# Latent attention with lookback: projection behind the second scores, mask on GpSimd, last key's values by DMA, two evictions on ScalarE

## The chip, the cores and the metric

The kernel runs on one core of one Trainium2 chip. The metric is the device time of one execution of the whole program, in microseconds (us); lower is better. Below, PE is TensorE, DVE is VectorE, ACT is ScalarE, POOL is GpSimd and SP is SyncE, as the profile names them.

## What is computed

The program is a stack of six layers on activations `x` of 64 x 32 tokens of 256 features: an adapter attention, a self attention, a ternary feed-forward, the latent attention that the change is about, a gated attention and a layer of experts. Only the fourth is touched. For each of the 64 batches it takes 32 query tokens and 257 context tokens (`ctx_2048`), 16 heads, and computes, with the context as 257 keys:

```python
kv_c = kv @ W_kvc                     # 256 -> 64
q_c = q @ W_dq                        # 256 -> 96
q_nope, q_rope = q_c @ W_uq, rope(q_c @ W_qr)
k_nope, v, k_rope = kv_c @ W_uk, kv_c @ W_uv, rope(kv_c @ W_kr)
scores = (q_nope . k_nope + q_rope . k_rope) / sqrt(192)
good = (k_ids <= seg_id) & (k_ids >= seg_id - 8)
attn = softmax(where(good, scores, -1e30))
out = (attn @ v) @ W_o
```

The up-projections of keys and values are folded into those of the queries and of the output, so that a batch has one key tile of 128 rows (64 of the latent, 64 rotary) and its values are the latent rows themselves, turned. All of it is in fp32.

## The kernel before

The order of work is written out by hand, engine by engine, with semaphores; there is no planner. `latent_attention` (line 1149) holds one function for each engine: `sp`, `pool`, `scalar`, `vector`, `tensor`. After a prologue (weights, folding, norm of x, latent queries `d_qcT`), all of them walk through 64 steps, one for a batch `b`, by `steps` (line 1234): steps 0 to 3 and 52 to 63 written out, 4 to 51 in a loop of eight steps. Four batches are a tile of 128 rows of x; the 16 heads are four groups, scored two at a time (u = 0 and u = 1). Every engine takes its instructions strictly in the order of its queue, and a wait holds all that is behind it.

TensorE's step b (line 1602) is in this order: first scores of b (L1566); second half of the weighting of b-2 (L1582); turning the first two groups' probabilities of b-1 (L1548); `values` of b, which turns the latent keys into values by two transposes (L1537) and copies the last key to four rows by a small product (L1539); keys of b+1 (L1515); in every fourth step (b mod 4 = 1, from 5) the output projection `project` of the tile before (L1591, 16 passes); second scores of b (L1566); `turn_last` of b-1, the last key's probabilities (L1556); queries of b+5 (L1525); turning the second two groups of b-1 (L1548); and the weighting of b-1, which starts with the last key (L1577) and then takes the first half (L1582). Keys and queries go through one bank of PSUM, so the queries of b+5 wait until VectorE has taken the keys of b+1 out.

VectorE's step (line 1439) makes the mask of the batch (`window`, L1434, from the distances of ScalarE), takes out the first scores with mask and maximum (L1421, L1423, negated maximum L1427), evicts the values (`values_out`: L1396 for the 256 keys, L1397 for the last key spread over a 4 x 4 diagonal), takes the keys of b+1 out with their rotary parts (L1375, L1377), takes out the second scores (L1427 again), adds the projection to x in every fourth step (L161 and the statistics L135), evicts the last key's turned probabilities (`last_out`, L1405) and takes the queries of b+5 out (L1386, L1388).

ScalarE's step (line 1325): exponentials of the first two groups (L1335), scaling of the second two groups of b-1 (L1316), output of b-2 out of PSUM (L1324), turned probabilities of b-1 out (L1309), exponentials of the second two groups, turned probabilities again, scaling of the first two groups of b, distances of b+1 (L1301). GpSimd adds the rotary halves of keys (L1251) and queries (L1256). SyncE loads the context of b+2 when the keys of b have left its buffer (L1230, in a loop).

In TensorE's queue `turn_last(b - 1, 1 - j, b)` waits for the values of b to have been evicted, and the weighting waits for the last key's probabilities:

```python
            def turn_last(b, j, values):
                pe.wait_ge(scaled.sem, scaled.at(b, 2))
                pe.wait_ge(v_out.sem, v_out.at(values, 1))
            ...
            def weigh(b, j, u):
                if u == 0:
                    pe.wait_ge(t3_out.sem, t3_out.at(b, 1))
```

Of the kernel before, what the change touches and what calls it, by code (L numbers as in the profile page):

```python
# [83 lines left out]
def build(nc, d, out):  # L84
# [1064 lines left out]
    def latent_attention(sb):  # L1149
# [20 lines left out]
        own3 = sb("d_own3", [G1, G1])  # L1170
# [7 lines left out]
        wm = sb("d_wm", [P, LC])  # L1178
# [11 lines left out]
        w_loaded = shared("w_loaded", 16 * 14, 1)  # L1190
# [4 lines left out]
        ctx_loaded = [shared(f"ctx_loaded{j}", 16, B // 2) for j in range(2)]  # L1195
        k_psum, k_half, k_ready = shared("k_psum", 1, B), signal("d_k_half"), signal("d_k_ready")
# [5 lines left out]
        wm_link, dist_ready = chain("d_wm_link", 1), signal("d_dist_ready")  # L1202
# [15 lines left out]
        def sp(eng):  # L1218
            for dst, name in ((wdq[:], "d_wdq"), (wuq[:], "d_wuq"), (wuk[:], "d_wuk"), (wuv[:], "d_wuv"),
                              (wo[:], "d_wo"), (wkvcT[:], "d_wkvcT"), (wkr[:], "d_wkr"),  # L1220
                              (qw[:, :, KVC:P], "d_wqr"), (own3[:], "d_own3"),
# [5 lines left out]
            with eng.Fori(1, B // 2) as i:  # L1227
                for j in range(2):
                    eng.wait_ge(k_psum.sem, k_psum.at(i * 2 + (j - 1), 0))
                    eng.dma_start(cT[j][:, :, :], d["ctx"][i * 2 + j]).then_inc(ctx_loaded[j].sem, 16)  # L1230
# [15 lines left out]
        def pool(eng):  # L1246
            low = slice(KVC, P)

            def key_sum(b, j):
                eng.wait_ge(k_half.sem, k_half.at(b, 1))  # L1250
                eng.tensor_tensor(kc[j][low, :], kc[j][low, :], ks[low, :], ALU.add).then_inc(k_ready.sem, 1)  # L1251

            def query_sum(n, s, g):

                eng.wait_ge(q_half.sem, q_half.at(n, 1))
                eng.tensor_tensor(qc[s][low, g, :, :, :], qc[s][low, g, :, :, :], qs[low, :, :, :], ALU.add)\  # L1256
                    .then_inc(q_ready.sem, 1)

            def step(b, s, tile, pair):
                if not (isinstance(b, int) and b == B - 1):  # L1260
                    key_sum(b + 1, (s + 1) % 2)
                if not (isinstance(b, int) and b >= B - AHEAD):
                    query_sum(b + AHEAD, (s + AHEAD) // BT % 2, (s + 1) % BT)

            key_sum(0, 0)
            for piece in range(AHEAD):
                query_sum(piece, piece // BT, piece % BT)
            steps(eng, step)

        def scalar(act):  # L1270
# [27 lines left out]
            def distances(b, j, first):  # L1298
                if not first:
                    act.wait_ge(wm_link.sem, b - 1)  # L1300
# [11 lines left out]
            def scale(b, j, u):  # L1312
# [4 lines left out]
                ins.then_inc(scaled.sem, 1)  # L1317

# [34 lines left out]
            for u in range(2):  # L1353
                turn_out(B - 1, u)
            output_out(B - 1, 7, NT - 1)

        def vector(dve):
# [5 lines left out]
            seg_link.link(dve, dve.tensor_scalar(segf[:, :], segf[:, :], LOOKBACK / 2, -1.0, ALU.subtract, ALU.mult))  # L1363
            with dve.Fori(0, NT // 2) as i:
# [27 lines left out]
            def values_out(b, j, first):  # L1392
                dve.wait_ge(v_psum.sem, v_psum.at(b, 1))
                if not first:
                    dve.wait_ge(pv_psum.sem, pv_psum.at(b - 1, 0))
                dve.tensor_copy(vc[j][:, :, :], ps[:, T_BANK[1], P:2 * P].rearrange("p (c e) -> p c e", c=2))  # L1396
                dve.tensor_tensor(v3[j][:, :, :], spread(ps[0:G1, T_BANK[1], 2 * P:2 * P + KVC], 1, G1),  # L1397
# [1163 lines left out]
```

## Time and profile before

| what | value |
| --- | --- |
| median of 3 runs | 3097.93 us (3092.5 to 3103.39) |
| the profiled execution's own time | 3107.65 us |
| its span, first to last instruction | 3105.8 us |
| granted TensorE clock over the span | 0.859 |
| fourth layer, from its first weight load to its last statistics | 1494 to 2211 us |
| its 64 steps, from the first to the last first-scores eviction | 1572 to 2197 us |

A row of a group of instructions has: line, engine, operation, out<-in by the program's names, shapes, count | busy us, mean ns of one | idle time of the engine before them and what ended it. A row of the timeline has: start, duration, engine, line, operation, names, count, and in brackets the idle time before it and what released it. The granted clock is 1.00 at 2.4 GHz and 0.50 at 1.2 GHz.

### The profile page before, as it was taken

The numbers are of one execution on the slowest core, as the hardware profiler recorded it, in microseconds if no ns is written. First come the engines' busy times: TensorE is split into PE (matmuls) and PEld (weight loads), VectorE is DVE, ScalarE is ACT, GpSimd is POOL, SyncE is SP. The second block draws the span as 40 slices with busy tenths as digits, with TensorE's granted clock in tenths as the row PEclk, the third lists the DMA queues.
The fourth block names the chain that finished last, engine by engine and source line by source line (L and its number), as shares of the span: only waits on it lengthen the run. The fifth ranks groups of instructions, "written<-read, shape, count | busy, mean of one in ns | idle before, by whom it ended". The sixth has DMA issues, their size and how long they took to land.

```text
span 3105.8 us, 53176 instructions
## 1 busy us (share of the span) xinstructions
PE 2305.6 (74%) x15563; PEld 1566.6 (50%) x15596; DVE 2027.5 (65%) x5626; ACT 1390.6 (45%) x3648; POOL 585.0 (19%) x634
## 2 busy tenths in 40 slices
PE   5699999999999783232578888888777445566555
PEld 4666666666666552111356666666555322233222
DVE  3356666666666455666267777776377787777777
ACT  1054555544554343232235555555455544444444
POOL 0011111111111000111021222211144442222222
PEclk9999999999999896676789999999778657766777
DMA  2010100000000001000201011011000220000000
GB/s 79 0 25 24 23 24 24 24 24 24 24 24 9 15 0 51 0 0 0 75 21 28 28 28 26 26 27 28 20 10 10 90 79 1 1 1 1 1 1 28
DMA packets 62257, 71.38 MB, mean 23 GB/s; under 512 B 39802, under 2 KB 41275, under 8 KB 59580
## 3 DMA queue, kind: packets, MB, share of 16 engines
q1 hardware_dynamic: 62140, 70.20, 7.7%
q14 instruction: 89, 0.73, 0.1%
q8 instruction: 28, 0.46, 0.1%
HBM read 63.20 MB, written 2.10 MB: 21 GB/s over the span
## 4 chain that ended last, share of the span: by engine, by line
PE 47%; issue 23%; DVE 19%; ACT 7%; DMA 1%; DVEq 1%; SPq 1%; POOL 1%; ACTq 0%; POOLq 0%
PE ps L613 5%; PE ps L660 5%; PE ps L591 4%; PE ps L600 4%; PE ps L627 4%; PE ps L563 2%; DVE d_st L1423 2%; PE ps L1945 2%; PE ps L1120 2%; PE ps L672 1%; ACT d_pr L1316 1%; PE ps L671 1%; DVE x_all L161 1%; PE ps L861 1%; PE ps L1566 1%
## 5 line engine op out<-in xcount | busy, mean ns | idle before, releaser
L350 ACT ACTIVATE a_pr<-ps,a_nm 128x257 f32<-128x257 f32 x512 | 238.1, 472 | 253.0 <-DVE a_nm L464 253.0
L1335 ACT ACTIVATE d_pr<-d_st,d_nm 128x257 f32<-128x257 f32 x256 | 128.2, 502 | 308.5 <-DVE d_nm L1427 305.3
L473 DVE COPY a_pT<-ps 128x512 f32<-128x512 f32 x256 | 176.3, 689 | 126.4 <-PE ps L627 126.4
L2385 PE MATMUL ps<-f_wt,f_nhT 128*128 128x256 bf16 x512 | 106.3, 347 | 170.6 <-DVE x_all L2285 168.9
L2142 POOL TENSOR_TENSOR f_rg<-f_rg 128x512 f32<-128x512 f32 x128 | 134.3, 1049 | 437.2 <-ACT f_rg L2174 430.5
L613 PE MATMUL ps<-a_kT,a_qbd 32*128 32x289 f32 x1024 | 205.5, 448 | 1.9 <-ACT a_pr L350 0.8
L2376 PE MATMUL ps<-f_wt,f_nxT 128*128 128x512 bf16 x480 | 186.9, 525 | 6.1 <-DVE f_act L2310 2.6
L2385 PEld LDWEIGHTS ps<-f_wt,f_nhT 128*128 128x128 bf16 x512 | 53.7, 117 | 256.6 <-issue 218.7
L2180 ACT ACTIVATE f_nhT<-ps 128x512 bf16<-128x512 bf16 x128 | 76.3, 596 | 231.0 <-PE ps L2394 231.0
L464 DVE TENSOR_REDUCE a_nm<-ps 128x2 f32<-128x514 f32 x256 | 174.9, 683 | 0.0
L660 PE MATMUL ps<-a_pT,a_v 128*32 128x128 f32 x2048 | 161.5, 279 | 0.9 <-DVE a_pT L473 0.9
L461 DVE SCALAR_TENSOR_TENSOR a_sf<-ps,a_amask 128x64 f32<-128x64 f32 x256 | 56.9, 222 | 155.4 <-PE ps L613 155.4
L627 PE MATMUL ps<-ident,a_pr 128*128 128x128 f32 x1024 | 157.1, 276 | 0.0
L1566 PE MATMUL ps<-d_kc,d_qc 128*128 128x257 f32 x512 | 148.0, 414 | 0.0
L2310 DVE TENSOR_TENSOR f_act<-ps,f_rg 128x512 f32<-128x512 f32 x128 | 88.6, 692 | 90.8 <-POOL f_rg L2142 68.1
L591 PE MATMUL ps<-a_cT,a_wqk 128*128 128x257 f32 x512 | 145.4, 406 | 2.2 <-DVE a_k L438 1.7
L627 PEld LDWEIGHTS ps<-ident,a_pr 128*128 128x128 f32 x1024 | 122.1, 140 | 45.1 <-issue 25.2
L290 POOL TENSOR_TENSOR a_sf<-a_sf,a_ratio 128x256 f32<-128x256 f32 x64 | 39.3, 614 | 515.2 <-DVE a_ratio L494 515.2
L1256 POOL TENSOR_TENSOR d_qc<-d_qc,d_qs 64x512 f32<-64x512 f32 x64 | 82.6, 1290 | 269.2 <-DVE d_qs L1388 269.2
L1112 PE MATMUL ps<-ident,c_nx 128*128 128x128 bf16 x64 | 9.7, 307 | 161.6 <-DVE c_nx L1049 161.6
L600 PE MATMUL ps<-a_wvg,a_cT 128*128 128x256 f32 x512 | 127.6, 392 | 0.0
L660 PEld LDWEIGHTS ps<-a_pT,a_v 128*32 128x32 f32 x2048 | 92.8, 109 | 57.4 <-issue 55.6
(349 smaller groups left out, 5887.3 us busy)
## 6 DMA issues: line engine op xcount, KB each, us to landing
a_cT<-in_ctx SPq DMA_DIRECT2D x64, 257.0 KB, 2.7
d_cT<-in_ctx SPq DMA_DIRECT2D x64, 257.0 KB, 2.6
f_wf<-in_f_w SPq DMA_DIRECT2D x12, 1024.0 KB, 4.8
a_vbd<-a_vself SPq DMA_DIRECT2D x256, 8.0 KB
e_vb<-e_vs SPq DMA_DIRECT2D x256, 8.5 KB
c_wf<-in_c_w SPq DMA_DIRECT2D x3, 1024.0 KB, 6.9
x_all<-in_x SPq DMA_DIRECT2D x1, 2048.0 KB, 7.7
d_wo<-in_d_wo SPq DMA_DIRECT2D x1, 2048.0 KB
```

The lines of the kernel that those rows point to most:

```text
L350: ins = act.activation(pr[j][:, g, :], ps[:, S_BANK[u % 2] + k, S:LK], ACT.Exp, bias=nm[j][:, g:g + 1], accum_out=ssum[j][:, 0, g:g + 1])
L464: dve.tensor_reduce(nm[j][:, 2 * u:2 * u + 2], ps[:, s0:s0 + 2, S:LK], AX.X, ALU.max, negate=True).then_inc(max_ready.sem, 1)
L473: dve.tensor_copy(pT[u % 2][:, :, :, :], ps[:, bank, :].rearrange("p (g c q) -> p g c q", g=2, c=2))\
L591: ins = pe.matmul(ps[:, P_BANK, 0:LC], lhsT=wqk[:, 2, k, m * P:m * P + P], rhs=cT[j][:, k, :], start=(k == 0), stop=(k == KT - 1))
L600: ins = pe.matmul(ps[:, P_BANK, c * HID:c * HID + HID], lhsT=cT[j][:, k, c * P:c * P + P], rhs=wvg[:, k, :], start=(k == 0), stop=(k == KT ...
L613: ins = pe.matmul(ps[:, S_BANK[u % 2] + k, 0:LK], lhsT=qbd[j][rows(g), g // HA, :, :].rearrange("p h q -> p (h q)"), rhs=kT[j][rows(g), g ...
L627: ins = pe.transpose(ps[:, T_BANK[1 if u == 1 else 0], (2 * k + c) * P:(2 * k + c + 1) * P], pr[j][:, 2 * u + k, c * P:c * P + P], ident[: ...
L660: ins = pe.matmul(ps[rows(g), O_BANK, m * P:m * P + P], lhsT=v[j][:, c, g * S:g * S + S], rhs=pT[u % 2][:, k, c, :], start=(m == 0 and c = ...
L1566: ins = pe.matmul(ps[:, S_BANK[u] + k, 0:LC], lhsT=qc[s // BT][:, g, s % BT, :, :].rearrange("p h q -> p (h q)"), rhs=kc[j][:, :], start=T ...
L2142: eng.tensor_tensor(rg2[j][:, :], rg[j][:, :], rg[j][:, :], ALU.mult).then_inc(sq_done.sem, 1)
L2376: ins = pe.matmul(ps[:, 2 + 2 * j + w, :], lhsT=nxT[s][:, k, :], rhs=wt[:, 3 * e + w, k * IE:k * IE + IE], start=(k == 0), stop=(k == KT - 1))
L2385: ins = pe.matmul(ps[:, 7, 0:HID], lhsT=nhT[k2 % 2][:, k, :], rhs=wt[:, 3 * (k2 % NE) + 2, k * HID:k * HID + HID], start=(k == 0), stop=(k ...
```

## The change

- TensorE: `project` moves from before the second scores to behind the queries of b+5. The wait behind it for the statistics of the tile becomes a wait for the addition to x alone. `values` loses its third product.
- Last key's values: 64 x 4 rows of last context tokens (`d_ctail`, 256 KB) are loaded with the weights, projected once for all batches in the prologue (4 products into PSUM), spread by VectorE into `v_tail` (2 operations of 128 x 256), and brought to `v3` for each batch by a DMA of SyncE (4 partitions of 1 KB). SyncE's loop is written out; in it the DMA of `v3` waits for the weighting of b-2, and the context load of the next step stands behind it.
- Mask: `window` moves from VectorE to GpSimd, for b+1, into two buffers. GpSimd waits for the distances of b+1 ahead of its key sum. ScalarE makes the distances of b+1 behind the scaling in the middle of the step, not at its end.
- Evictions: `values_out` (without the last key) and `last_out` move from VectorE to ScalarE, the one behind the first turned probabilities, the other behind the second exponentials.
- GpSimd's key and query sums work on all 128 partitions in place of 64; the rows of zeros that this needs are set once.

```diff
+            eng.wait_ge(vt_ready.sem, vt_ready.at(1, 0))
+            for b in range(B):
+                j = b % 2
+                if 1 <= b < B - 1:
+                    eng.wait_ge(k_psum.sem, k_psum.at(b, 0))
+                    eng.dma_start(cT[1 - j][:, :, :], d["ctx"][b + 1]).then_inc(ctx_loaded[1 - j].sem, 16)
+                if b >= 2:
+                    eng.wait_ge(pv_psum.sem, pv_psum.at(b - 1, 0))
+                at = G1 * (b % 32)
+                eng.dma_start(v3[j][:, :, :], v_tail[at:at + G1, b // 32, :, :]).then_inc(v3_loaded[j].sem, 16)
...
+            def window_wait(b):
+
+                eng.wait_ge(dist_ready.sem, dist_ready.at(b, 1))
+                if not (isinstance(b, int) and b < 2):
+                    eng.wait_ge(masked.sem, masked.at(b - 1, 0))
+
+            def window(b, j):
+                eng.tensor_scalar(wm[j][:, :], dist[j][:, :], LOOKBACK / 2, NEG, ALU.is_gt, ALU.mult)\
+                    .then_inc(wm_ready.sem, 1)
 
             def step(b, s, tile, pair):
                 if not (isinstance(b, int) and b == B - 1):
+                    window_wait(b + 1)
                     key_sum(b + 1, (s + 1) % 2)
+                    window(b + 1, (s + 1) % 2)
                 if not (isinstance(b, int) and b >= B - AHEAD):
                     query_sum(b + AHEAD, (s + AHEAD) // BT % 2, (s + 1) % BT)
...
+            def values_out(b, j, first):
+                act.wait_ge(v_psum.sem, v_psum.at(b, 1))
+                if not first:
+                    act.wait_ge(pv_psum.sem, pv_psum.at(b - 1, 0))
+                act.activation(vc[j][:, :, :], ps[:, T_BANK[1], P:2 * P].rearrange("p (c e) -> p c e", c=2), ACT.Copy)\
+                    .then_inc(v_out.sem, 1)
+
+            def last_out(b, first=False):
+
+                act.wait_ge(t3_psum.sem, t3_psum.at(b, 1))
+                if not first:
+                    act.wait_ge(pv_psum.sem, pv_psum.at(b - 1, 1))
+                act.activation(pT3[:, :], ps[0:G1, T_BANK[1], 0:P], ACT.Copy).then_inc(t3_out.sem, 1)
...
                     if u == 0 and not (isinstance(b, int) and b == 0):
                         scale(b - 1, 1 - j, 1)
+                    if u == 0 and not (isinstance(b, int) and b == B - 1):
+                        distances(b + 1, 1 - j, isinstance(b, int) and b == 0)
                     if u == 0 and not first:
                         output_out(b - 2, (s - 2) % 8, tile - (1 if s % BT < 2 else 0))
+                    if u == 1 and not (isinstance(b, int) and b == 0):
+                        last_out(b - 1, first)
                     if not (isinstance(b, int) and b == 0):
                         turn_out(b - 1, u, first)
+                    if u == 0:
+                        values_out(b, j, first)
                 scale(b, j, 0)
-                if not (isinstance(b, int) and b == B - 1):
-                    distances(b + 1, 1 - j, isinstance(b, int) and b == 0)
...
+            dve.wait_ge(vt_psum.sem, vt_psum.at(0, 1))
+            for c in range(2):
+                dve.tensor_tensor(v_tail[:, c, :, :], spread(ps[:, P_BANK, c * KVC:c * KVC + KVC], 1, G1),
+                                  spread(own3[:, :], 2, KVC), ALU.mult).then_inc(vt_ready.sem, 1)
             with dve.Fori(0, NT // 2) as i:
...
             def step(b, s, tile, pair):
                 j, n = s % 2, b if isinstance(b, int) else BT
-                window(b, j, n == 0)
-                scores_out(b, 0, n == 0)
+                scores_out(b, j, 0, n == 0)
                 if n > 0:
                     recip(b - 1, 1 - j, 1)
-                values_out(b, j, n < 2)
                 if n < B - 1:
                     keys_out(b + 1, 1 - j, n == 0)
                 recip(b, j, 0)
-                scores_out(b, 1, n == 0)
+                scores_out(b, j, 1, n == 0)
...
             pe.wait_ge(fold_out.sem, fold_out.at(0, 1))
+            for c in range(2):
+                for k in range(KT):
+                    ins = pe.matmul(ps[:, P_BANK, c * KVC:c * KVC + KVC], lhsT=ctail[:, k, c * P:c * P + P],
+                                    rhs=kw[:, k, 0:KVC], start=(k == 0), stop=(k == KT - 1))
+            ins.then_inc(vt_psum.sem, 1)
...
                 if n < B - 1:
                     keys(b + 1, 1 - j, pair)
-                if s % BT == 1 and n > 1:
-                    project(tile - 1, (s - BT) % 8 // BT, b - 1)
                 score(b, j, 1, s, n == 0)
                 if n > 0:
                     turn_last(b - 1, 1 - j, b)
                 if n < B - AHEAD:
                     queries(b + AHEAD, (s + 1) % BT, tile + (2 if s % BT == BT - 1 else 1), b + 1)
+                if s % BT == 1 and n > 1:
+                    project(tile - 1, (s - BT) % 8 // BT, b - 1)
                 if n > 0:
                     turn(b - 1, 1 - j, 1)
                     if s % BT == 1 and n > 1:
-                        layer_wait(pe, 4, tile)
-                    weigh(b - 1, 1 - j, 0)
+                        pe.wait_ge(x_link.sem, tile + 3 * NT)
+                    weigh(b - 1, 1 - j, 0, pair)
```

## Rows read from the trace of the kernel before

**Rows 1.** The page's first lines: span, and each engine's busy time.
```profile
span 3105.8 us, 53176 instructions
PE 2305.6 (74%) x15563; PEld 1566.6 (50%) x15596; DVE 2027.5 (65%) x5626; ACT 1390.6 (45%) x3648; POOL 585.0 (19%) x634
```

**Rows 2.** Windows: stretch, length, busy (count) PE, PEld, DVE, ACT, POOL, clock, DMA share, GB/s.
```profile
1493.50:1510.70 17.20, 0.00 (x0) 0.02 (x1) 0.90 (x3) 0.00 (x0) 0.00 (x0) 0.50 0.89 310
1608.05:2090.82 482.77, 423.03 (x2736) 315.62 (x2735) 346.40 (x1176) 259.99 (x768) 96.84 (x96) 0.96 0.10 27
1737.06:1776.11 39.05, 34.02 (x231) 25.45 (x230) 28.80 (x98) 21.67 (x64) 8.07 (x8) 1.00 0.09 28
2090.82:2196.50 105.68, 94.06 (x599) 69.29 (x597) 67.91 (x259) 59.57 (x176) 17.09 (x18) 0.95 0.09 24
```

**Rows 3.** Timeline of step 6, from its first scores to those of step 7.
```profile
1627.38 1.13 PE L1566 MATMUL ps<-d_kc,d_qc 128*128 128x257 f32 x4
...
1629.83 0.51 ACT L1335 ACTIVATE d_pr<-d_st,d_nm 128x257 f32<-128x257 f32 x1 [2.18 <-DVE d_nm L1427]
...
1629.88 0.27 PE L1539 MATMUL ps<-ident,d_kc 64*4 64x64 f32 x2
1630.08 0.73 PEld L1515 LDWEIGHTS ps<-d_cT,d_kw 128*128 128x128 f32 x4
...
1630.83 0.89 ACT L1316 ACTIVATE d_pr<-d_pr,d_ri 128x257 f32<-128x257 f32 x2
...
1631.34 0.43 DVE L1375 TENSOR_TENSOR d_kc<-ps,d_krope 128x257 f32<-128x257 f32 x1 [0.55 <-PE ps L1515]
...
1631.89 0.58 ACT L1309 ACTIVATE d_pT<-ps 128x512 f32<-128x512 f32 x1
...
1632.71 1.16 PE L1525 MATMUL ps<-d_qcT,d_qw 96*128 x8 [0.52 <-DVE d_ks L1377]
...
1633.70 0.17 DVE L1427 TENSOR_SCALAR d_nm<-d_mx 128x2 f32<-128x2 f32 x1
...
1633.90 0.51 ACT L1335 ACTIVATE d_pr<-d_st,d_nm 128x257 f32<-128x257 f32 x1 [1.44 <-DVE d_nm L1427]
...
1634.23 0.71 PE L1577 MATMUL ps<-d_pT,d_v 4*128 4x128 f32 x4
...
1635.46 1.13 PE L1566 MATMUL ps<-d_kc,d_qc 128*128 128x257 f32 x4
```

**Rows 4.** Timeline of step 7, around its last key's turning.
```profile
1641.01 0.27 PE L1556 MATMUL ps<-ident,d_pr 128*4 128x128 f32 x1 [0.84 <-ACT d_pr L1316]
...
1641.15 1.15 PE L1525 MATMUL ps<-d_qcT,d_qw 96*128 x8
```

**Rows 5.** Sources: engine, names, count, ns min/median/max, first and last start.
```profile
L1434 DVE TENSOR_SCALAR d_wm<-d_dist x63: 295/791/1276, 1577.6 to 2195.3; 128x257 f32<-128x257 f32 x63
L1276 ACT ACTIVATE d_kw<-ps x1: 263/263/263, 1525.2 to 1525.2; 128x128 f32<-128x128 f32 x1
```

**Rows 6.** Waits, 1572 to 2210 us: who waited for whom, total, times, longest.
```profile
DVE d_wm L1434 <- ACT d_dist L1301: 37.4, 49, 2.7
```

**Rows 7.** Timeline of step 5, around its projection.
```profile
1619.13 3.72 PE L1591 MATMUL ps<-d_vo,d_ot 128*128 128x256 f32 x16 [1.92 <-ACT d_ot L1324]
...
1622.68 1.03 PE L1566 MATMUL ps<-d_kc,d_qc 128*128 128x257 f32 x4
...
1624.90 0.42 DVE L161 TENSOR_TENSOR x_all<-ps,x_all 128x256 f32 x1
```

**Rows 8.** Groups by line on GpSimd, over the whole span.
```profile
L2134 POOL TENSOR_SCALAR f_neg<-f_wf,f_ws 128x1024 f32<-128x1024 f32 x12 | 43.7, 3645 | 16.7 <-DVE f_ws L2209 16.7
L1251 POOL TENSOR_TENSOR d_kc<-d_kc,d_ks 64x257 f32<-64x257 f32 x64 | 46.4, 726 | 307.6 <-DVE d_ks L1377 307.6
```

**Rows 9.** DMA issues of the page: count, KB each, median us to landing.
```profile
d_cT<-in_ctx SPq DMA_DIRECT2D x64, 257.0 KB, 2.6
```

**Rows 10.** Timeline of the prologue: the first turned tile of x.
```profile
1527.32 0.44 PE L1486 MATMUL ps<-ident,d_xn 128*128 128x128 f32 x2 [3.04 <-ACT d_vo L1277]
```

More of the change, by code:

```diff
@@ L1177, in latent_attention @@
         dist = [sb(f"d_dist{j}", [P, LC]) for j in range(2)]
-        wm = sb("d_wm", [P, LC])
+        wm = [sb(f"d_wm{j}", [P, LC]) for j in range(2)]
         tick = sb("d_tick", [P, 1])
@@ L1195, in latent_attention @@
         ctx_loaded = [shared(f"ctx_loaded{j}", 16, B // 2) for j in range(2)]
+        v3_loaded = [shared(f"vb_loaded{j}", 16, B // 2) for j in range(2)]
+        vt_psum, vt_ready, zeroed = signal("d_vt_psum"), signal("d_vt_ready", 2), signal("d_zeroed", 2)
         k_psum, k_half, k_ready = shared("k_psum", 1, B), signal("d_k_half"), signal("d_k_ready")
@@ L1352, in scalar @@
             output_out(B - 2, 6, NT - 1)
-            for u in range(2):
-                turn_out(B - 1, u)
+            turn_out(B - 1, 0)
+            last_out(B - 1)
+            turn_out(B - 1, 1)
             output_out(B - 1, 7, NT - 1)
@@ L1390, in queries_out @@
                 ins.then_inc(q_half.sem, 1)
[L1392 to L1397, printed above, removed]
-                                  spread(own3[:, :], 2, KVC), ALU.mult).then_inc(v_out.sem, 1)
-            def last_out(b, first=False):
-                dve.wait_ge(t3_psum.sem, t3_psum.at(b, 1))
-                if not first:
-                    dve.wait_ge(pv_psum.sem, pv_psum.at(b - 1, 1))
-                dve.tensor_copy(pT3[:, :], ps[0:G1, T_BANK[1], 0:P]).then_inc(t3_out.sem, 1)
             def recip(b, j, u):
@@ L1414, in output, with scores_out @@
                 add_to_x(dve, n, t, ps[:, O_BANK, Y_AT:Y_AT + HID])
-            def scores_out(b, u, first):
+            def scores_out(b, j, u, first):
                 dve.wait_ge(score_psum.sem, score_psum.at(b, u + 1))
+                dve.wait_ge(wm_ready.sem, wm_ready.at(b, 1))
                 if not first:
@@ L1446, in step @@
                 recip(b, j, 0)
-                scores_out(b, 1, n == 0)
-                if s % BT == 1 and n > 1:
-                    output(tile - 1)
-                if n > 0:
-                    last_out(b - 1, n == 1)
+                scores_out(b, j, 1, n == 0)
                 if n < B - AHEAD:
@@ L1456, in step @@
                     queries_out(b + AHEAD, (s + AHEAD) // BT % 2, (s + 1) % BT, False)
+                if s % BT == 1 and n > 1:
+                    output(tile - 1)
             keys_out(0, 0, True)
@@ L1507, in keys @@
             def keys(b, j, pair, first=False):
+                if first:
+                    pe.wait_ge(vt_ready.sem, vt_ready.at(1, 0))
                 pe.wait_ge(ctx_loaded[j].sem, ctx_loaded[j].at(pair + 1, 0))
@@ L1605, in step @@
                     keys(b + 1, 1 - j, pair)
-                if s % BT == 1 and n > 1:
-                    project(tile - 1, (s - BT) % 8 // BT, b - 1)
                 score(b, j, 1, s, n == 0)
@@ L1612, in step @@
                     queries(b + AHEAD, (s + 1) % BT, tile + (2 if s % BT == BT - 1 else 1), b + 1)
+                if s % BT == 1 and n > 1:
+                    project(tile - 1, (s - BT) % 8 // BT, b - 1)
                 if n > 0:
```

52 lines of the change are left out of this document (23 added, 29 removed).

## The prediction

> **What bounds the kernel now.** I read the page's totals first: TensorE is busy 74% of the span, VectorE 65%, ScalarE 45% [rows 1]. Those are means over six layers, and only the fourth changes, so I went on to windows of its steps. Steps 4 to 51 are twelve tiles of four batches and take 482.77 us, 40.23 a tile; a tile in which the granted clock stayed at 2.4 GHz took 39.05 [rows 2]. In the loop TensorE is busy 423 of 483 us, VectorE 346, ScalarE 260 [rows 2]. The reader is to see that no engine is full: TensorE idles 12%. What sets the time is the chain that leads from one batch's first scores to the next's, so the timeline of a step must be followed, not the busy sums.
>
> I count from the start of the first scores of step 6 (1627.38). Keys start at 2.70, VectorE takes them out from 3.96, the second negated maximum starts at 6.32, the queries at 5.33, the last key's product at 6.85, and the next first scores at 8.08 [rows 3]. The queries waited for the rotary parts of the keys, because both use one bank: that is the cycle here. In step 7 (first scores at 1635.46) it is another: the last key's turning waits for ScalarE and starts at 5.55 [rows 4], since the mask had held the first scores' eviction back. The mask costs 0.295 to 1.276 us, median 0.791 [rows 5], and VectorE waited 37.4 us in total for the distances in front of it [rows 6]. In the projection step TensorE waited 1.92 us for the output copy, then 16 passes put the second scores 3.55 us later [rows 7].
>
> **The change part by part.**
>
> *Mask off VectorE.* It takes 0.3 to 1.3 us and its wait off the head of steps 7, 8 and 5, nothing from step 6, whose cycle it does not touch. On GpSimd the nearest row is 3645 ns for 1024 elements [rows 8], so about 0.91 us for 257; the ends are 0.3 (VectorE's lowest) and 3.6 (that whole row). Queued behind it is only the query sum; the key sum of 0.73 [rows 8] stands ahead of it. Distances now come from ScalarE at about 4.7, the rotary parts end at 5.1, so mask b+1 is ready at 5.1 + 0.7 + 0.9 = 6.8 and is wanted at about 10.2. It is hidden, and at the upper end (9.5) too. The spread of the mask's duration, 295 to 1276 ns [rows 5], is what two engines in each other's way look like. The Trainium skill (Perfetto Trace Analysis, Optimizing Scalar/DVE Operations) says that the two share an SBUF port and that moving work between them "might not help". If the loss, 0.5 us a batch between lowest and median, came back on the path, that would add 32 us; with 3.4 us in hand I add nothing.
>
> *Values and last key to ScalarE.* VectorE is relieved of four small operations, but it waits for TensorE's keys anyway. What counts is where the copies stand in ScalarE's queue. The nearest price is 0.26 us (128 x 128 from PSUM) [rows 5]; the ends are 0.17 and 0.40. First exponentials start at 2.45, as now. The turned probabilities now start at 4.51 [rows 3]; the distances put in front add 0.40, the copy of 0.58 follows with 0.5 until the next start, so the values' copy starts at 5.4, ends at 5.7, and the last key's turning, which waits for it, starts at 5.8. Queries follow 0.14 later [rows 4] at 5.94, and the last key's product could start 1.52 behind them [rows 3], at 7.46. The second wait is later still. Keys start at 2.70 less the dropped product's 0.20 (1629.88 to 1630.08) = 2.50; to VectorE 1.26; to the second negated maximum 2.36; 0.20 to the second exponentials; 1.00 for these (1629.83 to 1630.83) [rows 3]; now the last key's copy 0.26 and about 0.1 of handover. 2.50 + 1.26 + 2.36 + 0.20 + 1.00 + 0.36 = 7.68. From that product to the next first scores is 1.23 [rows 3]. **A step without projection is 8.91 us** at full clock, against 8.08 in step 6. Before, that copy was on VectorE, ahead of nobody's exponentials; now all of the second exponentials lie between first scores and first scores.
>
> *Projection.* Queries at 5.94, about 1.0 for them, projection at 6.94 without a wait (the output copy ended at about 5.1), its end 3.72 later at 10.66, about 0.15 of handover and 0.42 for the addition to x [rows 7], 0.1 of handover: the last key's product at 11.33, next first scores at **12.56**. Behind the projection stand the second turning and both weightings; ScalarE waits for them and has its scaling done at about 12.6, before it is wanted at 14.2.
>
> *Tile.* 3 x 8.91 + 12.56 = 39.29, against 39.05: +0.24, and +2.9 for twelve tiles. The two waits of the projection step are gone, and the new wait in each of three others gives it back. Slow-clock time I leave as it is (40.23 - 39.05 = 1.18 a tile).
>
> *Last eleven steps.* Now 105.68 us [rows 2], because they are tighter and from step 59 no queries fill them. The ScalarE chain does not shorten without queries: 8 x 8.91 + 3 x 12.56 = 108.96, and some 3 us for the lower clock (0.95) as now: +6, bounds +2 and +9. First four steps +1.
>
> *DMAs and SyncE.* 64 new transfers of 4 KB, issued once the weighting of b-2 is done, some 14 us ahead of their use; the row at hand lands 257 KB in 2.6 us [rows 9]. Behind each stands the context of b+2, now issued at about 1.8 of step b and wanted 9.6 us later: 7 us in hand. Nothing on the path; without that cover it would be up to 2.6 a batch.
>
> *Prologue.* 256 KB more at 310 GB/s [rows 2] is 0.8 us, with the issue 1.0. TensorE turned the first tile at 1527.32, right behind ScalarE's folding [rows 10]; now four products (8 passes of 0.13 by the dropped product of [rows 3], 1.05), 0.15, two VectorE operations of about 0.42, the first normalised tile 0.41 and 0.1 come before it, as VectorE's queue has them ahead of the normalisation: +2.6, at the lower clock +3.6. Together +3.6. The zeroing on GpSimd lies under the weight load. End of the layer +0.5.
>
> **Sum:** 3.6 + 1 + 2.9 + 6 + 0.5 = +14.0. On the profiled execution: 3105.8 + 14.0 = 3119.8 span, 3121.7 time. That execution is 9.7 us above the median of the runs shown, so I put the difference on the median: 3097.9 + 14.0 = **3111.9 us**. A measurement of this kernel can tell about 0.3% (9.3 us) from no change.
>
> **The rivals.**
>
> *The copies don't gate (faster).* If ScalarE hands both over in time, a step runs as the key bank allows: queries at 5.13, product at 6.65 to 6.8, step 8.0; projection step 11.6. Tile 35.6, -41 for twelve; last steps 8 x 8.0 + 3 x 11.6 + 3 = 101.8, -4; with the +5 fixed, -40: 3058. TensorE's 34.0 us busy in the 39.05 tile [rows 2] leave room for it. Against it stands the written order: both waits are in TensorE's queue and both copies behind work that now ends later. Chance 0.17.
>
> *Shorter handovers (no change).* Each of the walk's nine handovers could be 0.02 less, 0.2 a step over 60 steps: -12, giving 3100. Chance 0.20.
>
> *The clock falls oftener (slower still).* The loop's mean of 0.96 [rows 2] is 8% of it at 1.2 GHz, and that costs 14 us. After the change TensorE stands idle from 4.5 to 5.8 in every step, then does narrow work. If low-clock time doubles, +14 and +2 at the end: 3128. It decides once the loop's mean clock is under 0.94. The Trainium skill (TensorE: Matmul & The Clock Gate, A second HAM failure mode) says that short idle spells between groups of products are enough to make the clock go back and forth; the trace agrees that it falls with TensorE 88% busy. Against it: the longest idle spell, that before the projection, goes. Chance 0.18.
>
> *The mask is the bound (slower).* From a GpSimd mask of about 4.3 us on, VectorE would wait for it; at 6 us each step takes some 2 more, +120: 3220. Its whole-row bound is 3.6. Chance 0.04.
>
> **How the numbers follow.** My forecast, +6 to +22, has 0.41; three quarters of it lies above +9.3. Faster by over 0.3%: 0.17 and 0.03 of the handover case, 0.20. Within: 0.17 of that case and 0.10 of the forecast, 0.27. Slower: 0.31 + 0.18 + 0.04 = 0.53. The range runs from 3070, which takes a part of the faster case in, to 3140, the clock case with the upper bounds of tail and copies; about 0.19 is left out.
>
> **What would show it.** In the profile after: first scores 8.9 us apart; the last key's product (second of the weighting) released by ScalarE's copy, idle before it 0.2 to 0.3; the last key's turning released by ScalarE at 5.8; projection started without a wait; 12.6 for that step; GpSimd's mask near 0.9 us with nobody waiting; VectorE idle before the first scores; the first turned tile of x 3.6 later. The forecast is wrong if ScalarE's copies are not what ends TensorE's idle time, or if the mean clock moves by over 0.02.

## The result: 52 us slower, with the walk through the step right and the clock not

The changed kernel takes 3151.23 us (median of 4, 3148.78 to 3163.33) against 3098.9 us: ratio 1.0178, 95% interval 1.0146 to 1.0211. I had forecast 3111.9 us with a range to 3140. The sign was right, the size was not.

In the profiled execution the span is 3147.6 us, 41.8 more than [rows 1]. From the first weight load to the next layer's first load, the fourth layer went from 717.1 to 770.7 us, +53.7. The five layers that the change does not touch took 2377 us where they had taken 2389; over all profiled executions here they lie between 2377 and 2394, so layer times are compared below, and whole times only by their medians.

The windows of the changed kernel (stretch, length, busy of PE, PEld, DVE, ACT, POOL, granted clock, DMA): the loop's twelve tiles and the last eleven steps, which answer to the second and fourth rows of [rows 2], and between them one step of the loop at full clock.

```profile
1609.60:2127.90 518.30, 449.38 (x2639) 332.88 (x2639) 283.39 (x985) 276.68 (x864) 147.78 (x144) 0.88 0.09 25
1727.78:1736.86 9.08, 7.43 (x53) 5.52 (x51) 5.65 (x21) 5.73 (x19) 3.08 (x3) 1.00 0.12 29
...
2127.90:2244.00 116.10, 98.24 (x579) 72.06 (x578) 56.90 (x214) 63.38 (x198) 28.83 (x29) 0.90 0.09 24
```

The loop took 518.3 us instead of 482.8, +35.5, at a mean clock of 0.88 instead of 0.96. By the trace's clock events its time at 1.2 GHz went from 37.5 to 119.5 us, from 8% to 23% of it. The last eleven steps took +10.4, the first four +0.5, the prologue +3.6, and the end of the layer +3.6, at a mean clock of 0.82 where it had been 1.00.

One step at full clock, from its first scores to the next ones, answers to [rows 3] and [rows 4]. Timeline of the changed kernel, step 15:

```profile
1727.78 1.14 PE L1593 MATMUL ps<-d_kc,d_qc 128*128 128x257 f32 x4
...
1730.28 1.14 PE L1544 MATMUL ps<-d_cT,d_kw 128*128 128x257 f32 x4
1730.30 0.51 ACT L1375 ACTIVATE d_pr<-d_st,d_nm 128x257 f32<-128x257 f32 x1 [2.52 <-DVE d_nm L1462]
...
1731.54 0.43 DVE L1424 TENSOR_TENSOR d_kc<-ps,d_krope 128x257 f32<-128x257 f32 x1 [1.28 <-PE ps L1544]
...
1733.25 0.26 ACT L1349 ACTIVATE d_vc<-ps 128x128 f32<-128x128 f32 x1
...
1733.56 0.27 PE L1583 MATMUL ps<-ident,d_pr 128*4 128x128 f32 x1 [1.27 <-ACT d_vc L1349]
...
1733.67 1.15 PE L1554 MATMUL ps<-d_qcT,d_qw 96*128 x8
1733.81 1.08 POOL L1278 TENSOR_SCALAR d_wm<-d_dist 128x257 f32<-128x257 f32 x1
1733.90 0.33 DVE L1462 TENSOR_SCALAR d_nm<-d_mx 128x2 f32<-128x2 f32 x1
...
1735.26 0.25 ACT L1357 ACTIVATE d_pT<-ps 4x128 f32<-4x128 f32 x1
...
1735.64 0.70 PE L1605 MATMUL ps<-d_pT,d_v 4*128 4x128 f32 x4 [0.38 <-ACT d_pT L1357]
```

Read the brackets. TensorE stands idle 1.27 us until ScalarE has copied the values, at 5.78 of the step, and 0.38 us until ScalarE has copied the last key, at 7.86; the next first scores are at 9.08. That is the forecast's chain.

And here is where the time went that the chain does not hold, in step 16 of the same kernel, the part that ends with the next first scores:

```profile
1742.49 0.27 PE L1583 MATMUL ps<-ident,d_pr 128*4 128x128 f32 x1 [1.12 <-ACT d_vc L1349]
...
1744.57 0.80 PE L1605 MATMUL ps<-d_pT,d_v 4*128 4x128 f32 x4 [0.47 <-ACT d_pT L1357]
1745.30 1.12 PE L1610 MATMUL ps<-d_pT,d_vc 128*64 128x128 f32 x8
1746.35 2.08 PE L1593 MATMUL ps<-d_kc,d_qc 128*128 128x257 f32 x4
1748.36 0.69 PE L1610 MATMUL ps<-d_pT,d_vc 128*64 128x128 f32 x8
```

The window of the slow stretch, in the columns of [rows 2]:

```profile
1745.00:1748.41 3.41, 3.41 (x17) 2.02 (x15) 0.78 (x2) 0.79 (x2) 1.26 (x1) 0.51 0.00 0
```

The first scores take 2.08 us instead of 1.14. TensorE had stood idle, then worked on products with few rows or columns, and at 1745.05 the granted clock fell to 1.2 GHz for 3.4 us. It falls 20 times in the loop, 11 times in the kernel before. There each fall lasts 3.4 us; here twelve do, one lasts 6.8 and seven last 10.2. Nineteen of the 20 come in the same place, 5.7 to 6.5 us behind a first negated maximum, towards the end of the step's part from second scores to next first scores. The Trainium skill (TensorE: Matmul & The Clock Gate, A second HAM failure mode) describes such a falling back and forth with small idle spells, for another kernel; the trace agrees, with 20 falls and no idle spell of TensorE over 1.34 us in the loop.

### The profile page after: what moved, and what is told of

Read it like the earlier page. It is cut to its first block, busy times and chain, and to the rows that moved or that the text cites. A ratio compares the mean times of both kernels' runs of the same rounds, so it can differ in the third digit from the quotient of the medians.

```text
span 3147.6 us, 52810 instructions
## 1 busy us (share of the span) xinstructions
PE 2330.6 (74%) x15476; PEld 1580.4 (50%) x15476; DVE 1941.0 (62%) x5372; ACT 1413.5 (45%) x3776; POOL 655.0 (21%) x700
## 4 chain that ended last, share of the span: by engine, by line
PE 54%; issue 20%; DVE 16%; ACT 6%; DMA 1%; POOL 1%; SPq 1%; DVEq 1%; ACTq 0%; POOLq 0%
PE ps L613 5%; PE ps L660 5%; PE ps L591 4%; PE ps L600 4%; PE ps L627 4%; PE ps L1593 3%; PE ps L1610 3%; PE ps L1544 2%; PE ps L563 2%; PE ps L1619 2%; PE ps L1120 2%; PE ps L1973 2%; PE ps L1605 1%; PE ps L672 1%; DVE d_ks L1426 1%
## 5 line engine op out<-in xcount | busy, mean ns | idle before, releaser
L1593 PE MATMUL ps<-d_kc,d_qc 128*128 128x257 f32 x512 | 172.1, 468 | 0.0
L1263 POOL TENSOR_TENSOR d_kc<-d_kc,d_ks 128x257 f32<-128x257 f32 x64 | 46.6, 728 | 414.6 <-DVE d_ks L1426 412.2
L1593 PEld LDWEIGHTS ps<-d_kc,d_qc 128*128 128x128 f32 x512 | 110.5, 228 | 31.2 <-issue 14.8
```

The costliest lines, as they stand in the source:

```text
L1593: ins = pe.matmul(ps[:, S_BANK[u] + k, 0:LC], lhsT=qc[s // BT][:, g, s % BT, :, :].rearrange("p h q -> p (h q)"), rhs=kc[j][:, :], start=T ...
```

## The experiments

Two theories. **Clock:** the walk of the step is right at 2.4 GHz, and the surplus is TensorE at 1.2 GHz, because its part of the step from second scores to next first scores, already thin, got idle time put into it. **Path:** the copies on ScalarE, the mask on GpSimd or the moved projection hold TensorE longer than walked. All ratios are to the kernel before, with 95% intervals. Rows shown are the window of the twelve tiles of the loop in each kernel's profile, with the columns of [rows 2]. Steps are from first scores to next first scores, at full clock. In the diffs, `...` marks what is left out, and comments are added.

**Two products more ahead of the last key's turning.** They add TensorE work where it waits.

```diff
                 score(b, j, 1, s, n == 0)
+                pe.wait_ge(masked.sem, masked.at(b, 2))
+                for k in range(2):
+                    pe.matmul(ps[:, 1, 264:504], lhsT=kw[:, 0, :], rhs=krope[:, 0, 0:240], start=True, stop=True)
                 if n > 0:
                     turn_last(b - 1, 1 - j, b)
```

> The changed kernel, with two products more in every step of TensorE, between the second scores and the last key's turning, where it stands idle 1.1 to 1.3 us: 128 x 240 from two constants (folded weights, rotary table) into free columns of a bank that nobody reads then; their result is used by nobody. Clock theory (the time that the walk through the step did not give is TensorE at 1.2 GHz: 518 us for the loop's twelve tiles against 469 by the walk, mean granted clock 0.88 against 0.96 before): the extra work raises the mean clock of the loop above 0.94, a tile comes down from 43.2 towards 39.5 to 40.5 us, the whole to 3105 to 3125 us. Path theory (the two copies on ScalarE hold TensorE longer than walked, whatever the clock): extra products in idle time take nothing away, the tile stays at 43 or grows by up to 0.5, 3150 to 3160 us.

3105.1 us, ratio 1.0018 (1.0003 to 1.0033): 46 us less than the changed kernel, by doing more.

```profile
1610.51:2085.84 475.33, 436.43 (x2833) 336.26 (x2832) 284.20 (x984) 276.66 (x864) 147.67 (x144) 1.00 0.10 27
```

The mean clock is 1.00, with one fall, and a tile is 39.6. The wait for the values is still there, cut to 0.44 us by the work in front of it. Timeline of this kernel:

```profile
1702.40 0.97 PE L1637 MATMUL ps<-d_krope,d_kw 128*128 128x240 f32 x4
1703.81 0.27 PE L1583 MATMUL ps<-ident,d_pr 128*4 128x128 f32 x1 [0.44 <-ACT d_vc L1349]
```

The path theory in its plain form has fallen: at full clock the changed loop is as walked.

**One product more behind the second turning**, late in that part of the step.

```diff
                     turn(b - 1, 1 - j, 1)
+                    for k in range(1):
+                        pe.matmul(ps[:, 1, 264:504], lhsT=kw[:, 0, :], rhs=krope[:, 0, 0:240], start=True, stop=True)
```

(The wait of the run above stands ahead of `turn_last` here too.)

> The changed kernel with one product more (128 x 240, constants, result used by nobody) in every step, not ahead of the last key's turning but behind the second turning, where TensorE stands idle about 0.4 us for the last key's copy. At full clock it costs 0.05 to 0.15 a step (tile 39.3 to 39.7). If the clock falls because of the whole thin part of the step, from the second scores to the next first scores, it helps there too: mean clock above 0.94, 3105 to 3125 us. If only the idle spell ahead of the last key's turning counts, the clock stays near 0.88 and the time is 3150 to 3160 us.

3103.74 us, ratio 1.0012 (0.9998 to 1.0026), and no fall in the loop:

```profile
1614.91:2089.43 474.52, 414.59 (x2737) 311.86 (x2736) 284.14 (x984) 276.62 (x864) 147.65 (x144) 1.00 0.10 27
```

The wait for the values is as long as in the changed kernel, so it is not that spell by itself; a product in either place does. Timeline of this kernel:

```profile
1706.80 0.27 PE L1583 MATMUL ps<-ident,d_pr 128*4 128x128 f32 x1 [1.28 <-ACT d_vc L1349]
```

**The wait alone**, a control: the same wait, no product.

> A control for the two runs of the changed kernel with added products: the changed kernel with the wait that stood ahead of these (TensorE waits for the first scores' eviction before the last key's turning) and no product. That eviction ends at 2.3 us of the step and the wait stands at 4.5, so it holds nothing up. Clock theory: falls and time as in the changed kernel, mean clock of the loop 0.87 to 0.90, 3145 to 3160 us. If the wait, by another phase of the queues, was what helped, mean clock above 0.94 and 3100 to 3110 us.

3157.43 us, ratio 1.0201 (1.0174 to 1.0229), 22 falls. The products did it, not the wait.

```profile
1605.98:2130.88 524.90, 459.19 (x2639) 339.32 (x2639) 283.05 (x985) 276.67 (x864) 147.76 (x144) 0.87 0.09 25
```

**Both copies back on VectorE**, everything else as changed.

```diff
+                values_out(b, j, n < 2)          # VectorE, ahead of keys_out
...
                 scores_out(b, j, 1, n == 0)
+                if n > 0:
+                    last_out(b - 1, n == 1)      # VectorE
...
-                    if u == 1 and not (isinstance(b, int) and b == 0):
-                        last_out(b - 1, first)   # ScalarE
-                    if u == 0:
-                        values_out(b, j, first)  # ScalarE
```

> The changed kernel with both evictions back on VectorE: the values' copy before the keys of b+1, the last key's copy directly behind the second scores' eviction. Walk at full clock: last key's turning at 4.5, queries at 5.1, last key's product at 6.7, step 7.9 to 8.0, projection step 11.8, tile 35.5. Clock theory: with the idle stretch of 1.2 us gone the falls get rarer again, mean clock of the loop about 0.95, tile 36.5 to 37, whole 3055 to 3070 us. If the falls came from the moved projection and not from the stretch, mean clock stays near 0.88 and the tile at 39: 3090 to 3105 us. Path theory: everything gained is the copies', clock unchanged, about 3090.

3036.17 us, ratio 0.9796 (0.9764 to 0.9827), faster than each of the times that I had put down. A step is 7.8 to 8.2, the projection step 11.7, the tile 35.59 (walk at full clock: 35.5); the loop has no fall, where I had expected a mean clock of 0.95.

```profile
1608.99:2036.03 427.04, 401.33 (x2641) 300.71 (x2640) 302.69 (x1080) 261.38 (x768) 148.09 (x144) 1.00 0.11 30
```

Its step 14, TensorE's lines with first scores at 1697.79, shows no wait ahead of the turning, and none ahead of the last key's product; only the queries wait, for the key bank:

```profile
1702.31 0.27 PE L1596 MATMUL ps<-ident,d_pr 128*4 128x128 f32 x1
1702.92 1.16 PE L1567 MATMUL ps<-d_qcT,d_qw 96*128 x8 [0.34 <-DVE d_ks L1421]
1703.92 0.60 PE L1588 MATMUL ps<-ident,d_pr 128*128 128x128 f32 x4
1704.48 0.71 PE L1618 MATMUL ps<-d_pT,d_v 4*128 4x128 f32 x4
```

**The last key's copy alone back on VectorE** (the second hunk of the diff above).

> The changed kernel with the last key's eviction alone back on VectorE, directly behind the second scores' eviction; the values' stays on ScalarE. Walk: last key's turning still at 5.8, its product at 7.5, step 8.7, tile 38.6. The idle spell ahead of the turning stays, so by the clock theory the falls stay (mean 0.88 to 0.90) and the gain is only 0.4 a step: 3125 to 3145 us. If the wait ahead of the last key's product were what lets the clock fall, mean above 0.94 and 3095 us.

3084.39 us, ratio 0.9953 (0.9936 to 0.9971). Full-clock steps of 8.3 to 8.8 (walk: 8.7); five falls.

```profile
1611.13:2074.09 462.96, 404.41 (x2641) 305.80 (x2640) 292.95 (x1033) 269.89 (x816) 147.72 (x144) 0.97 0.10 28
```

I had expected the falls to stay, as the idle spell ahead of the turning stays (up to 1.34 us), and 3125 to 3145 us. Most went. So my idea of which gap matters was too narrow.

**The values' copy alone back on VectorE** (the first hunk).

> The changed kernel with the values' eviction alone back on VectorE; the last key's stays on ScalarE behind the second exponentials. Walk: last key's turning at 4.5, queries at 5.1, then idle from about 6.7 to 7.7 ahead of the last key's product, step 8.9, tile 39.1: as long as in the changed kernel, with the idle spell 1.7 us later and cut to 1.0. Clock theory: the stretch from second scores to next first scores is as long and as thin as before, so the falls stay: 3135 to 3155 us. If only the spell ahead of the last key's turning mattered, mean clock above 0.94: 3100 to 3110 us.

3172.56 us, ratio 1.0230 (1.0194 to 1.0266): the slowest of all, and above the 3135 to 3155 that I expected, although the turning no longer waits for the values. 24 falls.

```profile
1617.59:2144.28 526.69, 464.75 (x2638) 341.44 (x2636) 294.68 (x1033) 268.79 (x816) 147.89 (x144) 0.86 0.09 25
```

With the two runs before, this places the harm: of the two copies it is the last key's, behind the second exponentials, that costs most. It sets the step's length (about 9.1 with or without the other). The traces also show what it does to the part between the end of the second scores and the next first scores, in full-clock steps without projection: that part is 4.5 us with 1.7 idle in the changed kernel, 4.5 with 1.5 here, 4.0 with 1.2 with the last key's copy on VectorE, and 3.5 with 0.5 with both. The falls are 20, 24, 5 and 0. The late product cuts the idle time to 1.3 of 4.5, and leaves no fall. So idle time in this part goes with the falls, but not it alone (1.2 with five falls, 1.3 with none); what exactly decides is not shown.

**The projection alone**, in the kernel before.

```diff
-                if s % BT == 1 and n > 1:
-                    project(tile - 1, (s - BT) % 8 // BT, b - 1)
                 score(b, j, 1, s, n == 0)
...
                     queries(b + AHEAD, (s + 1) % BT, tile + (2 if s % BT == BT - 1 else 1), b + 1)
+                if s % BT == 1 and n > 1:
+                    project(tile - 1, (s - BT) % 8 // BT, b - 1)
                 if n > 0:
                     turn(b - 1, 1 - j, 1)
                     if s % BT == 1 and n > 1:
-                        layer_wait(pe, 4, tile)
+                        pe.wait_ge(x_link.sem, tile + 3 * NT)
```

VectorE's addition to x moves with it, from ahead of `last_out` to behind the queries.

> The kernel before with the projection alone moved behind the queries (VectorE adds it to x behind the queries' eviction, TensorE waits for the addition alone); mask, evictions and last key's values as before. Walk of the projection step: queries 5.3, projection 6.3, its end 10.05, addition 10.6, last key's product 10.7, next first scores 11.95, against 12.9 before; the three other steps as before: tile 38.1 at full clock, 3080 to 3090 us if the clock stays at 0.96. If the moved projection is what brought the falls of the changed kernel, mean clock of the loop about 0.90 and 3105 to 3120 us.

3066.24 us, ratio 0.9891 (0.9875 to 0.9908): 34 us less, below the 3080 to 3090 expected. The projection step is 12.0 to 12.2 (walk: 11.95), but before it was 13.9 from first scores to first scores at full clock: the 12.9 that I set against the walk is the time between two first negated maxima, so that I priced the gain at 0.95 a tile and it is 1.9. Tile 37.1; the eleven falls are gone as well.

```profile
1609.53:2055.02 445.49, 405.22 (x2736) 303.90 (x2735) 346.38 (x1177) 261.29 (x768) 95.77 (x96) 1.00 0.10 29
```

**The mask alone on GpSimd**, in the kernel before, with the sums on 128 partitions that stand with it.

```diff
-                window(b, j, n == 0)                      # VectorE
...
+                    window_wait(b + 1)                    # GpSimd, ahead of key_sum(b + 1)
...
+                    window(b + 1, (s + 1) % 2)            # GpSimd, behind it
...
+                    if u == 0 and not (isinstance(b, int) and b == B - 1):
+                        distances(b + 1, 1 - j, isinstance(b, int) and b == 0)
```

> The kernel before with the mask alone on GpSimd a batch ahead, the distances in the middle of ScalarE's step, and what this needs (GpSimd's sums on all 128 partitions); projection, evictions and last key's values as before. Walk: the mask no longer holds the first scores' eviction, steps of 8.1, projection step 13.3: tile 37.6 at full clock, 3070 to 3085 us. If the mask on GpSimd is late or slows VectorE down, a wait for GpSimd shows at the first scores' eviction and the time is not below 3095 us.

3084.77 us, ratio 0.9953 (0.9925 to 0.9981): 16 us less; steps of 8.0 to 8.2 and a projection step of 13.2 to 13.4, as walked, and two falls in the loop. Only the first step of each pass through the loop of eight is longer, mostly 8.7 to 8.9: VectorE stands idle some 1.5 us at the loop's turn, with nothing in the profile that it waits for. The tile is 38.2 (walk: 37.6), and the time stands at the upper edge of what I expected.

```profile
1606.97:2065.67 458.70, 409.56 (x2737) 306.60 (x2736) 317.99 (x1129) 259.94 (x768) 147.90 (x144) 0.99 0.10 28
```

**Projection and mask together**, in the kernel before.

> The kernel before with the projection behind the queries and the mask on GpSimd a batch ahead; evictions and the last key's values (by product and VectorE in every step) as before. Against the run with both evictions on VectorE it lacks the values by DMA alone: 0.2 us a step on TensorE, 0.35 on VectorE, and it saves the 3.6 us of prologue. Walk: step 8.1, projection step 12.0, tile 36.3: 3040 to 3052 us, mean clock 1.00. If the values by DMA carried more than that, above 3055 us.

3057.42 us, ratio 0.9861 (0.9832 to 0.9891), tile 36.6 (36.3 walked); 3040 to 3052 us had been expected. It is 21 us above the run with both copies on VectorE, from which it differs by the last key's values by DMA alone, with SyncE's loop written out for them. Of the 21, 12 are in the loop's twelve tiles (36.58 - 35.59), with one fall against none: a step without projection is 0.2 us longer, as much as the dropped product took, and the step behind the loop's turn 0.5 or more. And of the layer as a whole (662.9 against 650.7 us in the profiled executions) it is 12, the rest being in layers that neither touches. Settled is only the 12, about the 10 that I gave them.

```profile
1602.63:2041.59 438.96, 408.24 (x2737) 305.92 (x2736) 318.81 (x1129) 261.15 (x768) 147.58 (x144) 1.00 0.11 29
```

**The projection back at its old place**, in the run with both copies on VectorE.

> The kernel of the run with both evictions on VectorE, but with the projection at its old place, before the second scores. Walk: steps of 7.95, projection step 13.2, tile 37.0 against 35.6: 3055 to 3065 us at full clock. If the projection's new place is part of what keeps the clock up there (no fall in the loop in that run), falls come back and the time is above 3070 us.

3053.25 us, ratio 0.9847 (0.9831 to 0.9863), a little under what was walked: projection step 12.7 instead of 11.7, tile 36.6, no fall. Here the new place is worth 17 us, 12 of them in the loop and nothing there through the clock; in the kernel before it was worth 34, and of the 37 in that profile's loop 14 came through the clock (1.18 a tile).

**One product more in the kernel before**, behind the second scores, with the same wait ahead of it.

> The kernel before with one product more (128 x 240, constants, result used by nobody) in every step behind the second scores. Clock theory: the eleven falls of its loop go too, the loop comes from 482.8 us to twelve tiles of 39.05 and what the product costs in the projection step, where TensorE is behind (0.45 each, 5 us in all): about 475 us, 3088 to 3096 us in all. It prices the slow clock of the kernel before at some 14 us. If the clock there does not depend on such gaps, the time grows by 5 us or more.

3102.07 us, ratio 1.0005 (0.9989 to 1.0022). Missed: five falls are left of eleven, and what was gained in the loop (482.8 to 476.7) is not seen in the whole. All five lie in projection steps, 2.3 to 3.2 us behind the first negated maximum, at the end of the idle spell of 1.92 us ahead of the projection or just behind it, where no product was added. Before, five lay there too; the six that came behind the second scores, in the part that the product was put into, are gone.

```profile
1601.89:2078.63 476.74, 433.34 (x2832) 328.18 (x2831) 346.92 (x1176) 259.93 (x768) 96.99 (x96) 0.98 0.10 27
```

**A version that beats both**: both copies on VectorE, and in the prologue the spreading of the last keys' values behind the normalisation, with their four products behind the first two turned tiles (not shown in the cut).

```diff
             with dve.Fori(0, NT // 2) as i:
                 for j in range(2):
                     dve.wait_ge(xT_psum.sem, xT_psum.at(i * 2 + j - 1, 0))
                     normed(dve, xn[:, j, :], i * 2 + j).then_inc(xn_ready.sem, 1)
+            dve.wait_ge(vt_psum.sem, vt_psum.at(0, 1))
+            for c in range(2):
+                dve.tensor_tensor(v_tail[:, c, :, :], ...
```

> The kernel of the run with both evictions on VectorE, with the last keys' values of all batches spread by VectorE behind the normalisation of x and not ahead of it, and their four products behind the first two turned tiles of x. In the changed kernel this part of the prologue took 1.5 us more than before from the folding to the first turned tile, and 0.7 more from there to the first keys. Expected 1 to 2 us less than that run, 3033 to 3036 us, which is within what a comparison can tell; the steps as there, 35.6 a tile. If the spreading is on the way of the first keys instead, no gain.

3034.66 us, ratio 0.9785 (0.9755 to 0.9816). The reordering itself brought nothing that can be told from the run with both copies on VectorE: the time from the folding to the first turned tile shrank by 2.4 us and came back as 1.4 up to the first keys and 0.9 behind them. The gain against the kernel before, 65 us, is that of the projection, the mask and the last key's values, with the two copies left on VectorE, where the kernel before has them.

The falls, by the traces' clock events in the loop, beside the time of a tile:

| kernel | time us | tile us | mean clock | falls |
| --- | --- | --- | --- | --- |
| before | 3099 | 40.2 | 0.96 | 11 |
| changed | 3151 | 43.2 | 0.88 | 20 |
| changed, wait alone | 3157 | 43.7 | 0.87 | 22 |
| changed, two products early | 3105 | 39.6 | 1.00 | 1 |
| changed, one product late | 3104 | 39.5 | 1.00 | 0 |
| changed, values' copy on VectorE | 3173 | 43.9 | 0.86 | 24 |
| changed, last key's copy on VectorE | 3084 | 38.6 | 0.97 | 5 |
| changed, both on VectorE | 3036 | 35.6 | 1.00 | 0 |
| same, projection at its old place | 3053 | 36.6 | 1.00 | 0 |
| before, projection moved | 3066 | 37.1 | 1.00 | 0 |
| before, mask on GpSimd | 3085 | 38.2 | 0.99 | 2 |
| before, projection and mask | 3057 | 36.6 | 1.00 | 1 |
| before, one product more | 3102 | 39.7 | 0.98 | 5 |

## Why the prediction was wrong in size, by its own steps

*The step without projection: right.* Forecast at full clock 8.91, turning at 5.8, second negated maximum at 6.12, last key's product at 7.68. Measured 9.08, 5.78, 6.12 and 7.86. The 0.17 between is mostly the second negated maximum, 0.33 us instead of 0.17, in the step shown, when GpSimd's mask had just begun. Two sources of the changed kernel (count, ns min/median/max):

```profile
L1278 POOL TENSOR_SCALAR d_wm<-d_dist x64: 1082/1084/1102, 1552.4 to 2237.6; 128x257 f32<-128x257 f32 x64
```

```profile
L1462 DVE TENSOR_SCALAR d_nm<-d_mx x128: 168/169/427, 1573.1 to 2246.6; 128x2 f32<-128x2 f32 x128
```

In the kernel before, none of these took over 0.171 us from step 1 on. With the mask alone on GpSimd they reach 0.432. I had weighed whether the mask's loss beside GpSimd would only move with it, and added nothing, because GpSimd has time in hand. A part did come onto VectorE: 0.16 us a step, not the 0.5 that it would have been had the whole loss moved. The Trainium skill (Perfetto Trace Analysis, Optimizing Scalar/DVE Operations) says that the two engines share an SBUF port and that moving work between them might not help. Here it did help, by 16 us for the mask alone. That the port is the cause of the 0.16 was not tested by itself.

*The projection step: right within 0.4 us.* Forecast 12.56; 12.2 and 12.4 from first scores to first scores at full clock, in the run with two products more.

*The tile at full clock: right.* Forecast 39.29; 39.5 and 39.6 with the clock kept up by added products. That it is so near is in part luck: the three other steps are some 0.16 above the walk each, and the projection step 0.26 below it. The gain of the projection and of the mask was given back by the new waits, as forecast.

*The mask on GpSimd: right in its place.* 1.08 us against 0.91, nobody waits for it.

*DMAs and SyncE: right.* No wait for the context or the last key's values stands among the waits of the layer.

*The prologue: right in its sum, by terms that make up for each other.* Forecast +3.6; +3.9 up to the first keys, less 0.3 up to the first maximum. The weights' load took 1.7 more up to the folding (forecast 1.0; 0.6 to 1.2 in other profiles with that load), the way from there to the first turned tile 1.5 (forecast 2.6), and the way on to the first keys 0.7 (not in the sum). The recorded sum also has two figures for one term, 2.6 and "at the lower clock" 3.6; its +3.6 goes with the first. TensorE's first turned tile is now released by VectorE's normalisation, answering to [rows 10]:

```profile
1527.96 0.69 PE L1513 MATMUL ps<-ident,d_xn 128*128 128x128 f32 x2 [1.24 <-DVE d_xn L153]
```

*"Slow-clock time I leave as it is": this step failed.* It put 1.18 us a tile, 14 in the loop. In the changed kernel the loop takes 518.3 us and at full clock about 474.5 to 475.3, so the slow clock costs 43 to 44, 29 to 30 more than carried over. The loop was forecast +2.9 and came to +35.5: 6 at full clock, the other 29 by the clock. My own sign of a wrong forecast, a mean clock that moves by over 0.02, shows in the loop (0.96 to 0.88) and hardly over the whole span (0.859 to 0.850). The last eleven steps, forecast +6, came to +10.4 at a mean of 0.90, and the end, forecast +0.5, to +3.6 at 0.82. I had this as a rival, named its place and its test (a loop mean under 0.94; it is 0.88), gave it 0.18 and priced it at +14 in the loop for a doubling. The falls nearly doubled, 11 to 20, but eight of them last 6.8 or 10.2 us instead of 3.4, so time at 1.2 GHz tripled. Its price, 14 for the loop, was half of the 29 measured. What I should have read from [rows 3]: behind the second scores, all of TensorE's step but the second turning is products that use 4 to 96 rows, or 4 or 64 columns, of 128, and the change puts both its waits into just that part. By the traces, in steps without projection, it was 3.4 to 3.9 us long with 0.5 to 1.0 idle, and is 4.5 to 4.6 with 1.7 idle. That the clock stays up when work is put into this part is shown by the added products; whether the narrow products in it matter was not tested.

*Against it I had set that the idle spell ahead of the projection goes.* True: moving the projection alone takes all eleven falls away. But that spell was 1.92 us in one step of four, and the waits for the two copies are 1.27 and 0.38 us in the step shown. Nor does a spell ahead of the projection bring falls by itself: with both copies on VectorE and the projection at its old place it is up to 1.5 us, without a fall.

*The faster rival*, that the copies don't gate, was walked at a tile of 35.6 and 3058 us. As a kernel, with both copies on VectorE, it measures 35.59 and 3036. The tile was walked right at full clock; the sum had carried on the 14 us of slow clock in the loop, which are gone there.

## What to carry to other kernels

Before a small eviction is moved to a less busy engine, ask where it lands in that engine's queue and who is held up behind it: VectorE was not full, and the 0.25 us copy behind a pair of exponentials made every step 1.1 us longer (9.1 against 8.0 at full clock, with and without it). Where a kernel's matmuls sit in a chain with thin work at one end, walk the chain at full clock and then ask separately what idle time the change puts there; the mean granted clock of the stage that changed, not of the whole span, is the first row to compare. And separate a change of four parts into its parts before judging it: two of these (projection, mask) gain 34 and 16 us alone and 43 together, with the third (last key's values by DMA) 63, and the fourth (evictions) loses 115 against that.

## What the runs showed of the hardware that I had not expected

Work whose result nobody uses made the kernel 46 us faster, 3151 to 3105 us, by keeping TensorE's granted clock at 2.4 GHz (mean of the loop 0.88 to 1.00), and one product a step was enough (0.57 us for its two passes in the trace); the wait that came with it did nothing by itself (3157 us). A VectorE operation on two elements a partition took 0.33 us instead of 0.17 when it started beside a GpSimd operation of 1.08 us. And layers that the change does not touch took between 2377 and 2394 us in single profiled executions, a spread of 17 us (0.5% of the whole) that has to be kept apart before small differences are read.
